# A graph layer's kernel: zero stores and a clearing move, destination rows are spread by TensorE, GpSimd scales and adds the bias for two gate phases

## What is computed

```python
xn = layernorm(x)
xw = xn @ W                                   # 8 heads of 32
e  = leaky_relu(a_src[src] + a_dst[dst])      # per edge and head
gnn = relu(segment_sum(xw[src] * softmax_over_dst(e)) + bias)
x = x + gnn + mix(xn)                         # mix: linear attention with quadratic features, projected
x = x + ffn(layernorm(x))                     # ffn: 2 of 16 experts per row, softmax weights, layernorm
```

## Time and profile before

| | us |
|---|---|
| median of 3 runs (lowest, highest) | 3071.61 (3068.89, 3074.11) |
| the profiled execution | 3075.73 |
| its span, first to last instruction | 3074.0 |
| PE / DVE / ACT / POOL busy in it | 2528.0 / 2112.2 / 1434.7 / 1977.0 |
| mean granted TensorE clock, share of full | 0.916 |
| set-up ends / edge stage begins / gate begins / last scatter ends | 46.2 / 389.4 / 2355.8 / 2534.4 |

### The profile page before, as it was taken

The page is one execution under the profiler, slowest core; times in us unless marked ns, Lnnn a source line. Parts: engine busy times, 40 slices in busy tenths (PEclk is TensorE's granted clock), DMA queues, the critical chain, the costliest instruction groups (busy, mean ns, idle before and its releaser), DMA issues. The chain is left out here.

```text
span 3074.0 us, 52974 instructions
## 1 busy us (share of the span) xinstructions
PE 2528.0 (82%) x12108; PEld 1639.8 (53%) x12108; DVE 2112.2 (69%) x5060; ACT 1434.7 (47%) x3421; POOL 1977.0 (64%) x2089
## 2 busy tenths in 40 slices
PE   5999888889788978887888888797864528999996
PEld 2555445445445455544545454444443527888884
DVE  8888877777777777767777777777777834333335
ACT  3444465556555555555555646454532311222227
POOL 4666767777777777777777777777773571222224
PEclk9999999999998999999998989999986559999998
DMA  6222244554545454545455455444442165777777
GB/s 170 44 46 44 63 140 137 151 143 136 150 137 143 137 150 137 143 144 142 137 150 143 138 143 143 143 136 143 137 136 85 67 209 174 232 233 232 233 239 254
DMA packets 297444, 450.53 MB, mean 147 GB/s; under 512 B 116374, under 2 KB 193467, under 8 KB 297190
## 3 DMA queue, kind: packets, MB, share of 16 engines
q0 software_dynamic: 86320, 241.77, 27.8%
q1 hardware_dynamic: 183142, 134.74, 15.8%
q10 hardware_dynamic: 27744, 71.38, 7.0%
HBM read 393.49 MB, written 55.83 MB: 146 GB/s over the span
## 5 line engine op out<-in xcount | busy, mean ns | idle before, releaser
L216 POOL DMA_INDIRECT rows_g<-node_rows,idx x1564 | 1489.5, 952 | 483.4 <-issue 446.9
L1196 PE MATMUL p_m<-msg,sel 128*128 128x264 f32 x3512 | 986.2, 429 | 236.5 <-DVE msg L1164 191.8
L1196 PEld LDWEIGHTS p_m<-msg,sel 128*128 128x128 f32 x3512 | 688.3, 206 | 363.2 <-issue 252.5
L1164 DVE TENSOR_TENSOR msg<-rows_g,p_w 128x1024 f32<-128x1024 f32 x439 | 534.7, 1218 | 42.9 <-ACT p_w L1062 41.2
L1062 ACT ACTIVATE p_w<-lg 128x32 f32<-128x32 f32 x439 | 88.3, 201 | 721.7 <-DVE lg L1157 716.2
L1867 POOL DMA_INDIRECT moe<-ysb,token x120 | 116.3, 969 | 349.2 <-DVE ysb L1854 324.2
L1017 ACT ACTIVATE sel_t<-apart,ones 128x512 bf16<-128x512 bf16 x442 | 319.0, 722 | 31.2 <-issue 1.1
L1153 DVE TENSOR_TENSOR lg<-rows_g,ends 128x32 f32<-128x32 f32 x439 | 86.3, 196 | 352.7 <-SPq L996 249.4
L1086 DVE TENSOR_TENSOR sel<-p_w,dst_t 128x512 f32<-128x512 f32 x440 | 303.1, 689 | 21.8 <-issue 5.3
L1014 ACT ACTIVATE apart<-dst_all,iota_neg 128x512 bf16<-128x512 bf16 x442 | 312.5, 707 | 0.0
L1040 ACT ACTIVATE qfeat<-p_scr 128x512 f32<-128x512 f32 x442 | 239.5, 588 | 103.3 <-PE p_scr L1219 98.8
(11 more groups left out here) (340 smaller groups left out, 3323.0 us busy)
## 6 DMA issues: line engine op xcount, KB each, us to landing
dst_all<-dst_bc ACTq DMA_DIRECT2D x112, 512.0 KB, 4.2
wa<-in_L_ffn_w_dram SPq DMA_DIRECT2D x64, 512.0 KB, 4.8
wb<-in_L_ffn_w_dram SPq DMA_DIRECT2D x64, 512.0 KB, 5.3
rows_g<-node_rows,idx POOLq DMA_INDIRECT x1564
xs<-slot_x SPq DMA_DIRECT2D x56, 258.0 KB, 2.9
ya<-moe SPq DMA_DIRECT2D x48, 256.0 KB, 4.6
bb<-in_L_ffn_b_dram SPq DMA_DIRECT2D x64, 128.0 KB, 5.5
qs<-xn_turned ACTq DMA_DIRECT2D x13, 512.0 KB, 5.5
```

What stands on the lines that cost most here:

```text
L216: pool.indirect_dma_start(rows_g[:, j, u, :], None, node_rows, bass.IndirectOffsetOnAxis(ap=idx[q][:, j, u:u + 1], axis=0)).then_inc(gathe ...
L1164: dve.tensor_tensor(m4, g3[:, :, 0:D].rearrange("p u (h e) -> p u h e", h=H), p_w[:, 0:TC * H].rearrange("p (u h) -> p u h", u=TC).unsquee ...
L1196: mm = pe.matmul(p_m[j % 2][:, 0:ROW], sel[j][:, u, :], msg[j % 2][:, u, :], start=(u == 0), stop=(u == TC - 1))
```

## The change

In words, in the order of the code. Set-up: the six zero stores go from SP's queue to GpSimd's, behind VectorE's memsets; GpSimd's clearing of acc goes to the start of its node stage. dst_all (128 partitions) becomes dst_rows, of which two single rows are used; a row of ones is added, and `cast_rows` has TensorE multiply the row of ones (as weights, one row of 128) with a row of 512 places, which writes the places to all 128 partitions of the bank p_cast. ScalarE's Square reads that bank. To have the bank free, the two p_sp become one, and `spread` in the round of step s is that of step s + 1 and waits for the logits of step s (before: of step s + 2, with the same wait). Gate: phases of 4, 6, 6, 10, 12, 12 tiles in place of 4, 6, 10, 10, 10, 10; the sums of the first 16 tiles are inverted first; GpSimd then does product and bias of phases 1 and 2, and VectorE only the rest (`add_to_rows`).

```diff
-        dst_all = [sb(f"dst_all{i}", [P, R, TC * P], BF16, ctx=early) for i in range(2)]
+        dst_rows = sb("dst_rows", [C + 1, R, TC * P], BF16, ctx=early)
+        ones_bf = sb("ones_bf", [C + 1, P], BF16, ctx=early)
+        dst_row = [dst_rows[i * C:i * C + 1, :, :] for i in range(2)]
+        ones_row = [ones_bf[i * C:i * C + 1, :] for i in range(2)]
...
-            act.dma_start(dst_all[q][:].rearrange("p s e -> p (s e)"),
-                          dst_bc[bass.ds(s, R), :].rearrange("(a s) e -> a (s e)", a=1).broadcast_to([P, R * TC * P])).then_inc(dst_in[q], 16)
+            act.dma_start(dst_row[q].rearrange("p s e -> p (s e)"),
+                          dst_bc[bass.ds(s, R), :].rearrange("(a s) e -> a (s e)", a=1)).then_inc(dst_in[q], 16)
...
-                for t in range(T, TQ):
-                    sp.dma_start(xn_turned[t * P:(t + 1) * P, :], zrow[:]).then_inc(scratch_out, 16)
...
-                pool.memset(acc_flat[:, 2 * H * FEAT:T * ROW], 0.0)
+                pool.wait_ge(pads_set, 3)
+                for t in range(T, TQ):
+                    pool.dma_start(xn_turned[t * P:(t + 1) * P, :], zrow[:]).then_inc(b_in, 16)
...
+                dve.memset(ones_bf[:], 1.0)
...
+                pool.memset(acc_flat[:, 2 * H * FEAT:T * ROW], 0.0)
                 pairs(pool, T, body)
...
-            p_sp = [ps(f"p_sp{i}", [P, 512], c) for i in range(2)]
+            p_sp = ps("p_sp", [P, 512], c)
+            p_cast = ps("p_cast", [P, TC * P], c)
...
-                def select_turned(s, q, j):
-                    if j == 0:
-                        act.wait_ge(dst_in[q], (s - q * R) * (16 // R // 2) + 16)
-                    act.activation(apart[j % 2][:], dst_all[q][:, j, :], ACT.Square, bias=iota_neg[:])
+                def select_turned(s, j):
+                    act.wait_ge(dst_cast, s + 1)
+                    act.activation(apart[j % 2][:], p_cast[:], ACT.Square, bias=iota_neg[:])
...
+                def cast_rows(s, q, j):
+                    if j == 0:
+                        pe.wait_ge(dst_in[q], (s - q * R) * (16 // R // 2) + 16)
+                    wait(pe, sel_t_ready, s)
+                    pe.matmul(p_cast[:], ones_row[q], dst_row[q][:, j, :], start=True, stop=True).then_inc(dst_cast, 1)
+
                 def spread(s, j, b):
-                    wait(pe, logit_ready, s - 1)
+                    wait(pe, logit_ready, s)
                     pe.wait_ge(sel_t_ready, s + 1)
...
                 def body(s, k, n, last):
                     j = k % R
-                    b = block_of(s + 2)
+                    if s + 1 < STEPS:
+                        b = block_of(s + 1)
                     if not (isinstance(s, int) and s == 0):
                         aggregate(s - 1, (j - 1) % R)
+                    cast_rows(s + 3, (k + 3) // R % 2, (j + 3) % R)
                     if n is not None:
                         query(n, k)
-                    spread(s + 2, (j + 2) % R, b)
-
-                for j in range(2):
-                    spread(j, j, block_of(j))
+                    if s + 1 < STEPS:
+                        spread(s + 1, (j + 1) % R, b)
+
+                cast_rows(0, 0, 0)
+                spread(0, 0, block_of(0))
+                for j in range(1, 3):
+                    cast_rows(j, 0, j)
...
-        SPANS = ((0, 4), (4, 10), (10, 20), (20, 30), (30, 40), (40, T))
-        PHASES, TP = len(SPANS), 10
+        SPANS = ((0, 4), (4, 10), (10, 16), (16, 26), (26, 38), (38, T))
+        PHASES, TP = len(SPANS), 12
...
-                invert(*SPANS[0])
+                early = SPANS[2][1]
+                w = acc[:, 0:early, D:ROW]
+                dve.tensor_scalar(w, w, TINY, None, ALU.max)
+                dve.drain()
+                dve.reciprocal(w, w).then_inc(inverses_ready, 1)
+                dve.drain()
                 residual(0)
-                invert(SPANS[0][1], T)
+                invert(early, T)
...
-                for ph in range(1, PHASES):
+                dve.wait_ge(pool_made, 2)
+                add_to_rows(1)
+                norm(1)
+                choose(0)
+                place(0)
+                dve.wait_ge(pool_made, 3)
+                add_to_rows(2)
+                choose(1)
+                norm(2)
+                place(1)
+                for ph in range(3, PHASES):
                     residual(ph)
                     choose(ph - 1)
                     norm(ph)
...
+                pool.wait_ge(inverses_ready, 1)
+                for ph in (1, 2):
+                    lo, hi = SPANS[ph]
+                    a = acc[:, lo:hi, 0:D]
+                    a4 = a.rearrange("p t (h e) -> p t h e", h=H)
+                    pool.tensor_tensor(a4, a4, acc[:, lo:hi, D:ROW].unsqueeze(3).broadcast_to([P, hi - lo, H, C]), ALU.mult)
+                    pool.drain()
+                    pool.tensor_tensor(a, a, b_gnn[:].unsqueeze(1).broadcast_to([P, hi - lo, D]), ALU.add).then_inc(pool_made, 1)
```

More of the change, by code:

```diff
@@ L357, in _ @@
                              src[full * CHUNK:E].rearrange("(p u) -> p u", u=u4)).then_inc(tail_out, 16)
-                sp.wait_ge(scratch_out, (TQ - T + G4 + 1) * 16)
+                sp.wait_ge(scratch_out, (G4 + 1) * 16)
             @block.gpsimd
@@ L471, in _ @@
                 dve.scalar_tensor_tensor(out=nmr[:], in0=mv[:, :, 0], scalar=-1.0, in1=rstd[:], op0=ALU.mult, op1=ALU.mult)
-                dve.wait_ge(b_in, (3 + H + 1) * 16)
+                dve.wait_ge(b_in, (3 + H + 1 + TQ - T) * 16)
                 dve.tensor_scalar(t_col[:], t_col[:], SCALE * SCALE, None, ALU.mult)
@@ L909, in gps_layer @@
             sel_t_ready = sem("sel_t_ready", c)
+            dst_cast = sem("dst_cast", c)
             dst_spread = sem("dst_spread", c)
@@ L960, in slot_free @@
                 wait(act, feat_used, (n - back) * NF + (old + 1))
-            def p_e(j):
-                return p_sp[j % 2][:, 0:TC * 3 * 2 * H]
+            p_e = p_sp[:, 0:TC * 3 * 2 * H]
             def chunk_in(ch, j):
@@ L1064, in body @@
                     act.activation(msg[j % 2][:, :, D:ROW], lg[j % 2][:], ACT.Exp).then_inc(denom_ready, 1)
-                    select_turned(s + 3, (k + 3) // R % 2, (j + 3) % R)
+                    select_turned(s + 3, (j + 3) % R)
                     if j == 1:
@@ L1073, in _ @@
                 for j in range(3):
-                    select_turned(j, 0, j)
+                    select_turned(j, j)
                 rounds(act, body)
@@ L1146, in body @@
                     dve.wait_ge(dst_spread, s + 1)
-                    dve.tensor_reduce(ends[j % 2][:], p_e(j).rearrange("p (u r a) -> p u a r", u=TC, r=3), AXX, ALU.add)
+                    dve.tensor_reduce(ends[j % 2][:], p_e.rearrange("p (u r a) -> p u a r", u=TC, r=3), AXX, ALU.add)
                     dve.drain()
@@ L1169, in _ @@
                 rounds(dve, body)
-                dve.wait_ge(dst_spread, STEPS + 2)
                 for s in (STEPS - 2, STEPS - 1):
@@ L1179, in block_of @@
                     return pe.value_load(blk_row[0:1, bass.ds(s, 1)], min_val=0, max_val=T - 1)
+                def cast_rows(s, q, j):
[3 more added lines that the diff above has]
+                    pe.matmul(p_cast[:], ones_row[q], dst_row[q][:, j, :], start=True, stop=True).then_inc(dst_cast, 1)
                 def spread(s, j, b):
-                    wait(pe, logit_ready, s - 1)
+                    wait(pe, logit_ready, s)
                     pe.wait_ge(sel_t_ready, s + 1)
                     for u in range(TC):
-                        mm = pe.matmul(p_e(j)[:, u * 6 * H:(u + 1) * 6 * H], sel_t[j][:, u * P:(u + 1) * P],
+                        mm = pe.matmul(p_e[:, u * 6 * H:(u + 1) * 6 * H], sel_t[j][:, u * P:(u + 1) * P],
                                        adm_parts[:, bass.ds(b, 1), :, :].rearrange("p a r f -> p (a r f)"), start=True, stop=True)
@@ L1332, in gps_layer @@
             spread_e = sb("spread_e", [P, P], ctx=c)
-            own_set = sem("own_set", c)
+            pool_made = sem("pool_made", c)
+            inverses_ready = sem("inverses_ready", c)
             cnt = sb("cnt", [P, TP, NEXP], ctx=c)
@@ L1418, in residual, with add_to_rows @@
                     dve.drain()
+                    add_to_rows(ph)
+                def add_to_rows(ph):
                     for lo, hi in PARTS[ph]:
@@ L1443, in invert @@
                     dve.drain()
-                invert(*SPANS[0])
+                early = SPANS[2][1]
[4 more added lines that the diff above has]
+                dve.drain()
                 residual(0)
-                invert(SPANS[0][1], T)
-                dve.wait_ge(own_set, 1)
+                invert(early, T)
+                dve.wait_ge(pool_made, 1)
                 norm(0)
```

2 lines of the change are left out of this document (1 added, 1 removed).

## The result

The changed kernel takes **3081.63 us** (median of 7 runs, 3078.32 to 3087.13) against 3071.61 before: ratio 1.0035, 95% interval 1.0026 to 1.0044, which is 10.7 us slower (the ratio times 3071.6; the medians differ by 10.0). The forecast was 3077.3, "within 0.2%, on the slow side". The range (3062 to 3088) holds the result. The limit of 0.2% (6.1 us) was missed: the whole interval lies above it, and the sum (+5.7) is half of what came.

The account below looks back on a forecast made before the run. GpSimd's back-to-back gathers bound the edge stage, its scatters and waits for VectorE's places the gate. Set-up 0, edge middle 0, start +3.1, end -2.5, gate +5.1 sum to +5.7: 3077.3 us, range 3062 to 3088.

Parts of the forecast that it names:

- Set-up, 0: Set-up: between -1.5 and +3 us, taken as 0; VectorE starts earlier, but moved zero stores may delay x.
- Edge stage, middle, 0: Mid edge stage: TensorE's extra matmul, taken as 0.25 us, fits inside VectorE's 0.57 us slack per step; 0 us.
- Rival C: Edge stage: TensorE becomes the bound, in steps with two query pieces; 3129 us if steps grow by 0.7 us; 12%.
- Start, +3.1: Edge stage's start: first messages come later and GpSimd waits for them; between 0 and +5 us, taken as +3.1.
- Three waits: Edge stage's start: GpSimd's fifth, sixth and seventh chunks wait for messages 0, 1 and 2.
- End, -2.5: Edge stage's end: a 512 KB broadcast before the last gather becomes 16 KB; last chunk arrives 2.5 us sooner.
- Gate, +5.1: Gate: -5.0 us if GpSimd and VectorE don't disturb each other, +5.1 if they take turns at SBUF; +5.1 taken.
- Turns: Gate: VectorE's two-input SBUF instructions stand still while GpSimd's four TENSOR_TENSORs run, 10.1 us in all.
- first places: Gate: VectorE's first scatter places for GpSimd, forecast near 2392 us with turns, 2382 without.
- fourth places: Gate: VectorE's places for GpSimd's fourth phase of scatters, at 2443.3 us without turns; GpSimd waits 8.8 us for them.
- B: Rival, gate: no turns, VectorE's products run on beside GpSimd's; sum -4.4 us, 3067 us; 28%.
- D: Rival: set-up gives 4 us or more as x lands earlier, edge start costs nothing; some -9 us, 3063; 12%.

Follow-up runs that it names:

- e5_order: The kernel before with only the edge stage's part of the change, TensorE's spread of the next step moved ahead of the queries' matmuls; ratio 1.0014 (1.0004 to 1.0023).
- e8_spans: The kernel before with the gate's new phases and VectorE order, product and bias of phases 1 and 2 kept on VectorE; ratio 1.0017, +5.2 us.

## Why the prediction was right, and where it was not

**The result's side and range** were right; "within 0.2%" was not, and the sum was 5.7 where 10.7 was measured. Of the missing 5.0 us, 3.4 belong to the edge's part by the run with that part alone (4.0 for 0.6), which has two mis-sized terms, the middle and the start.

**Set-up, 0**: +0.6 (-2.1 to +3.4) measured. The number held, a reason did not: the stores were priced, and x is late without them. That is luck in part.

**Edge stage, middle, 0**: this is the step that failed. "Inside 0.57 us per step" compares averages, and the cast took 0.40 us, not 0.25. The stalls are 0.8 to 8 us in the six profiles with that part, and none in the eight without. They need both things that the change does to TensorE: a bank of look-ahead less (alone: no stall) and a matmul more (alone: no stall). They follow stretches at the low clock. That the lost bank was the cushion for these stretches fits VectorE's waits for one spread (none in the kernel before, up to 3.8 us in the changed kernel), but e5_order stalls without such waits, so by which path the delay comes is argued and not shown. Rival C had the place right and the price wrong: not every step, only those stretches.

**Start, +3.1**: 5.1. Three waits as reasoned, and step 1's reduction comes 4.4 us later as forecast (11.9 us after the table load, 7.6 before). The fourth wait, at 437.36, was left out, and the clock took nothing back: from 420 to 430 us it was 0.84, 1.00 before.

**End, -2.5**: -2.3 in the profile after. In the six profiles with this part the gate begins 9.2 to 10.6 us after the last gather, in the eight without it 11.1 to 13.0 (12.9 in the kernel before).

**Not in the sum**: about -3 in the node stage. With it the edge's part comes to 5.1 + 0.8 to 8 - 2.4 - 3, that is 0.5 to 8; 4.0 was timed. The profiles bound the middle no better than that.

**Gate, +5.1**: +5.8 timed (2.8 to 8.6), +6.7 in the profile. Turns 9.7 us for 10.1 (the prediction's own terms, 12 less 1.4 and 0.1, are 10.5 and not 10.1; it changes nothing here); first places 2390.5 with the gate 1.8 us earlier, for 2392; fourth places 2452.0, where 2443.3 + 10.1 - 1.8 is 2451.6. B is refused by the rows. But what the step didn't say plainly is in e8_spans: nearly the same loss stands without turns and without help, because the phases, with their order on VectorE, cost 5 alone. The step had it in its arithmetic (8.8 us of waiting for the fourth places) and hid it in a net figure.

**D** is refused: the set-up gave nothing, and the start cost 5.1 us.

## What to carry to other kernels

Before spending a spare buffer on a new intermediate, price the buffer: look for the slowest stretches (here steps of 9.4 us with TensorE at the low clock) and ask how many steps the consumer is covered there, not how much it waits on average. When a producer works in phases with one phase of look-ahead, the consumer's end is the last phase that it waits for plus the rest of its own work, so a later, larger phase can undo an earlier gain; and work lent to GpSimd is worth only what is left after VectorE has stood still for it (here 9.7 us).

## What the runs showed of the hardware that was not expected

- GpSimd's gathers ran at one of two mean spacings that differ by 0.2%, 1.2532 (nine profiles) or 1.2504 us (five), from the stage's start to its end; over 1,564 gathers that is 4 us.
- The same node-stage matmuls lost 6.1 to 6.4 us to "issue" in eight programs and 0.6 to 0.7 in six, which differ elsewhere.
- Beside a clearing by GpSimd, which reads nothing, VectorE's one-input instruction of 392 elements took 5.90 us (0.35 in the kernels without the clearing there). It began 1.4 us ahead of the clearing and ended 0.2 behind it. In the node stage of the changed kernel a 50-element one took 1.53 us (0.18 before), and ended with the clearing.
